# Routing work of batch 6 moved among the last batch's attention steps

## The reference, cut to what matters

```
x = x + tanh(g_xattn[0]) * retention(layernorm(x), ctx)          # stages F (front)
x = x + tanh(g_ffn[0])   * (relu(x W_up) W_down + expert mix)     # stages F
x = x + tanh(g_xattn[1]) * attention(layernorm(x), ctx, ctx)      # stages T, for the last batch L
x = x + tanh(g_ffn[1])   * (shared(x) + top 6 of 64 experts(x))   # stages R route, then the experts

# attention: 8 batches, 8 heads of 32 x 512
sm  = softmax(einsum('bdm,bdn->bmn', qh, kh) * scale)
ret = einsum('bmn,bcn->bcm', sm, vh)
# last layer, for each token:
scores = sigmoid(layernorm(x) @ w_gate); top 6; weights; position in the expert's queue (CAP 256)
```

## Time and profile before

| | us |
|---|---|
| median of 3 runs | 1052.45 |
| lowest, highest of them | 1051.8, 1053.76 |
| the profiled execution | 1051.3 |
| its span, first to last instruction | 1049.5 |
| PE busy in it | 990.5 |
| DVE, ACT, POOL busy | 603.0, 335.0, 465.1 |

### The profile page before, as it was taken

The page is one execution under the profiler, slowest core; times in us unless marked ns, Lnnn a source line. Parts: engine busy times, 40 slices in busy tenths (PEclk is TensorE's granted clock), DMA queues, the critical chain, the costliest instruction groups (busy, mean ns, idle before and its releaser), DMA issues.

```text
span 1049.5 us, 15353 instructions
## 1 busy us (share of the span) xinstructions
PE 990.5 (94%) x5629; PEld 603.6 (58%) x5630; DVE 603.0 (57%) x1249; ACT 335.0 (32%) x491; POOL 465.1 (44%) x457
## 2 busy tenths in 40 slices
PE   7999989999999999999999998895999999999886
PEld 6986545564564564464465452344777777776432
DVE  3334554765765855746756747543655556553566
ACT  3411024124133233323333231442444434443221
POOL 2000025526557467477467544352355555556000
PEclk9999999999999999999999999898999999999999
DMA  8793279697680590680610409356899999965998
GB/s 321 284 385 127 103 256 332 222 357 293 232 327 28 209 336 1 234 311 1 238 68 32 152 32 363 153 206 265 303 373 387 371 370 368 371 255 208 380 417 322
DMA packets 93622, 262.23 MB, mean 250 GB/s; under 512 B 10454, under 2 KB 10582, under 8 KB 92784
## 3 DMA queue, kind: packets, MB, share of 16 engines
q1 hardware_dynamic: 43760, 146.18, 38.0%
q10 hardware_dynamic: 31872, 63.97, 16.3%
q0 software_dynamic: 17920, 51.15, 12.4%
HBM read 129.91 MB, written 139.72 MB: 257 GB/s over the span
## 4 chain that ended last, share of the span: by engine, by line
PE 68%; DVE 8%; POOL 7%; DMA 7%; issue 6%; ACT 2%; SPq 0%; POOLq 0%; ACTq 0%; DVEq 0%
PE banks L1273 17%; PE banks L1892 11%; PE banks L1283 10%; DMA e_eo<-y_d 6%; PE banks L1881 6%; PE banks L1901 6%; POOL t_psum L773 5%; PE banks L1391 5%; PE banks L1453 5%; DVE t_nmx L1064 2%; PE banks L1471 2%; ACT t_probs L864 2%; DVE t_nmx L1073 1%; PE banks L1265 1%; PE banks L1456 1%
## 5 line engine op out<-in xcount | busy, mean ns | idle before, releaser
L1715 POOL DMA_INDIRECT y_d<-e_eo,e_ids x128 | 124.5, 973 | 126.3 <-DVE e_eo L1812 93.6
L1064 DVE TENSOR_REDUCE t_nmx<-banks 128x4 f32<-128x2048 f32 x56 | 128.1, 2287 | 58.3 <-PE banks L1391 58.3
L773 POOL TENSOR_TENSOR t_psum<-t_psum,t_probs 128x512 f32<-128x512 f32 x104 | 128.7, 1268 | 61.9 <-ACT t_probs L864 61.0
L864 ACT ACTIVATE t_probs<-banks 128x2048 f32<-128x2048 f32 x56 | 105.2, 1878 | 139.7 <-PE banks L1456 115.8
L785 POOL DMA_INDIRECT xs_d<-r_norm,r_xaddr x96 | 95.9, 998 | 49.2 <-issue 24.9
L1453 PE MATMUL banks<-b_qry,b_key 32*128 32x512 f32 x512 | 73.9, 647 | 7.9 <-ACT t_probs L864 5.7
L743 POOL TENSOR_TENSOR f_rstd<-f_veps,mhalf 128x2 f32<-128x2 f32 x24 | 16.8, 699 | 144.2 <-DVE f_veps L962 144.2
L1881 PEld LDWEIGHTS banks<-ident,e_xg 128*128 128x128 f32 x512 | 56.9, 143 | 34.3 <-issue 34.1
L1881 PE MATMUL banks<-ident,e_xg 128*128 128x128 f32 x512 | 63.9, 280 | 12.5 <-DMA e_xg<-xs_d 12.5
L773 POOL TENSOR_TENSOR t_psum<-t_probs,t_probs 128x512 f32<-128x512 f32 x52 | 66.5, 1316 | 12.4 <-ACT t_probs L864 6.3
L1391 PE MATMUL banks<-b_key,b_qry 32*128 32x512 f32 x448 | 63.9, 639 | 3.7 <-DVE t_nmx L1064 2.0
(11 more groups left out here) (227 smaller groups left out, 1646.7 us busy)
## 6 DMA issues: line engine op xcount, KB each, us to landing
xs_d<-zero ACTq DMA_DIRECT2D x32, 1056.0 KB, 7.1
e_xg<-xs_d SPq DMA_DIRECT2D x32, 1056.0 KB
y_d<-zero ACTq DMA_DIRECT2D x24, 1024.0 KB, 7.5
e_xg<-y_d SPq DMA_DIRECT2D x16, 768.0 KB, 14.8
e_eo<-y_d SPq DMA_DIRECT2D x16, 768.0 KB, 14.4
wo<-in_wud SPq DMA_DIRECT2D x6, 768.0 KB, 11.9
wupT<-in_wud SPq DMA_DIRECT2D x6, 768.0 KB, 11.7
a_x<-in_x SPq DMA_DIRECT2D x8, 512.0 KB, 4.7
```

The lines of the kernel that those rows point to most:

```text
L773: ins = g_.tensor_tensor(psum0[:, q, :], first[:, q, :], probs[s % NP][:, q, :], ALU.add)
L864: A(probs[s % NP][:, :, :], quad[:, :, :], ACT.Exp, scale=SCALE1).then_inc(W["exp_ok"], 1)
L1064: V.tensor_reduce(nmx[g][:, m, :], quad[:, :, :], axis=AX.X, op=ALU.max, negate=True).then_inc(W["mx_ok"], 1)
L1715: g_.indirect_dma_start(out=y_d, out_offset=bass.IndirectOffsetOnAxis(ap=ids[:, HC * p + n:HC * p + n + 1], axis=0), in_=eo[u][:, n, :], i ...
```

## The change

The table `ENDING` has the routing of batch 6 at other places, two entries of `CHOSEN` go, so that `R.turnA/6` and `R.turnB/6` take work banks of the rotation instead of pV's and a chosen one, and the first `L.V` of batch 7 waits for the copy of `L.up0` (the last user of pV's bank now) instead of for that of `R.turnA/6`. No instruction is added or removed.

- `R.stats/6` and `R.norm/6` stood ahead of the maxima of `L.S5` and of `L.S7`; they stand behind `L.P1/7` on DVE.
- `R.turnA/6`, `R.turnB/6` stood ahead of `L.Q0/7`; they stand behind `L.V0/7`.
- `R.gates/6` stood behind `L.Q0/7`; it stands behind `L.V1/7`. `R.pos/6` stood behind `L.Q2/7` and `L.M1/7`; it stands behind `L.V2/7`.
- `L.Q1/7` stands directly behind `L.Q0/7`.

```diff
-L.S1b/7 L.S2/7 L.V6/6 L.V7/6 T.cT/7 T.A1/6 L.up0a/7 T.add1/6 R.x1/5 L.S3a/7 L.S4/7 L.S3b/7 L.up0b/7 L.P0/7 R.x2/5 R.stats/6 L.S5/7 L.S6a/7 L.M0/7 L.up0c/7 L.up0d/7
-R.norm/6 L.S7/7 L.S6b/7 R.turnA/6 R.turnB/6 R.x3/5 R.acc/5 R.acc/6 L.P1/7 L.Q0/7 R.gates/6 R.keep/6 L.Q1/7 L.V0/7 R.top/6 L.Q2/7 L.M1/7 R.pos/6 L.V1/7 L.Q3/7
...
+L.S7/7 L.S6b/7 R.x3/5 R.acc/5 R.acc/6 L.Q0/7 L.P1/7 R.stats/6 R.norm/6 L.Q1/7 L.V0/7 R.turnA/6 R.turnB/6 L.Q2/7 L.M1/7 L.V1/7 R.gates/6 R.keep/6 L.Q3/7 R.top/6
+L.V2/7 R.pos/6 R.slots/6 R.x0/6 R.weigh/6 R.x1/6 R.x2/6 L.Q4/7 L.V3/7 L.A0/7 L.add0/7 L.stats0/7 R.x3/6 L.Q5/7 L.V4/7 L.norm0/7 L.Q6/7 L.V5/7 L.turn0/7 L.Q7/7 L.gates0/7 L.top0/7
...
-CHOSEN = {("L.V4", 6): 2, ("L.up0a", 7): 3, ("L.M0", 7): 2, ("R.turnA", 6): 3, ("R.turnB", 6): 2}
+CHOSEN = {("L.V4", 6): 2, ("L.up0a", 7): 3, ("L.M0", 7): 2}
...
-                    pe.wait_ge(W["x4T_ok"], 2 * b - 1)
+                    pe.wait_ge(W["raw_ok"], 1)
```

More of the change, by code:

```diff
@@ L449 @@
 F.down0/7 T.sum0c/6 T.Q5/6 F.down1/7 T.Q6/6 T.V3/6 T.Z0/6 T.Q7/6 F.stats3/7 R.x3/4 F.norm3/7 T.A0/6 L.V4/6 L.S0/7 L.S1a/7 L.V5/6 T.add0/6 R.x0/5
-L.S1b/7 L.S2/7 L.V6/6 L.V7/6 T.cT/7 T.A1/6 L.up0a/7 T.add1/6 R.x1/5 L.S3a/7 L.S4/7 L.S3b/7 L.up0b/7 L.P0/7 R.x2/5 R.stats/6 L.S5/7 L.S6a/7 L.M0/7 L.up0c/7 L.up0d/7
-R.norm/6 L.S7/7 L.S6b/7 R.turnA/6 R.turnB/6 R.x3/5 R.acc/5 R.acc/6 L.P1/7 L.Q0/7 R.gates/6 R.keep/6 L.Q1/7 L.V0/7 R.top/6 L.Q2/7 L.M1/7 R.pos/6 L.V1/7 L.Q3/7
-R.slots/6 R.x0/6 R.weigh/6 L.V2/7 R.x1/6 R.x2/6 L.Q4/7 L.V3/7 L.A0/7 L.add0/7 L.stats0/7 R.x3/6 L.Q5/7 L.V4/7 L.norm0/7 L.Q6/7 L.V5/7 L.turn0/7 L.Q7/7 L.gates0/7 L.top0/7
+L.S1b/7 L.S2/7 L.V6/6 L.V7/6 T.cT/7 T.A1/6 L.up0a/7 T.add1/6 R.x1/5 L.S3a/7 L.S4/7 L.S3b/7 L.up0b/7 L.P0/7 R.x2/5 L.S5/7 L.S6a/7 L.M0/7 L.up0c/7 L.up0d/7
+L.S7/7 L.S6b/7 R.x3/5 R.acc/5 R.acc/6 L.Q0/7 L.P1/7 R.stats/6 R.norm/6 L.Q1/7 L.V0/7 R.turnA/6 R.turnB/6 L.Q2/7 L.M1/7 L.V1/7 R.gates/6 R.keep/6 L.Q3/7 R.top/6
+L.V2/7 R.pos/6 R.slots/6 R.x0/6 R.weigh/6 R.x1/6 R.x2/6 L.Q4/7 L.V3/7 L.A0/7 L.add0/7 L.stats0/7 R.x3/6 L.Q5/7 L.V4/7 L.norm0/7 L.Q6/7 L.V5/7 L.turn0/7 L.Q7/7 L.gates0/7 L.top0/7
 L.V6/7 L.pos0/7 L.slots0/7 L.rows0a/7 L.V7/7 L.up1/7 L.A1/7 L.up2/7 L.add1/7 L.stats1/7 L.rows0b/7 L.norm1/7 L.turn1/7 L.gates1/7 L.top1/7 L.pos1/7 L.slots1/7 L.rows1/7
```

## The result

The changed kernel takes 1066.36 us (median of 4, 1064.57 to 1067.76) against 1052.22: ratio 1.0135, interval 1.0113 to 1.0158. That is slower, as forecast, but 14 us instead of 4.8, and outside the range. A second measurement of the same kernel gave 1063.57 us and 1.0114 (1.0092 to 1.0136). The profiled execution is the slowest of the first four: 1067.76 us, span 1066.0.

What follows compares the result with a forecast made beforehand. PE, busy 94% of the span, was taken as the bound, beside a path through POOL's queue with 0.74 us to spare. 1.6 + 1.7 + 1.5 = 4.8 us on 1052.45 gave 1057.3 us, range 1053.8 to 1060.0 (8 in 10).

Steps and rivals of the forecast that it cites:

- the maxima's gain at `L.Q0`: On DVE, moments and norm leave the maxima: `L.Q0` starts at 662.4 us against 664.71, a gain of 2.3 us.
- the positions' lateness: PE reaches the positions of batch 6 at 678.3 us, so its addresses are out at 679.7, 2.3 us later.
- the gap ahead of L1503: PE stands idle for 4.6 us ahead of the turn of the last batch's first half.
- The rival in which PE alone sets the end: POOL's rows do not gate the turn, PE's gain of 2.9 us goes through: 1049.5 us; chance of faster 0.04.
- that in which the clock never falls: Gaps of 2.0 and 4.6 us on PE leave the clock alone, only +1.6 us remains: 1054.1 us; chance 0.17.
- step 6: PE's clock falls to half near `L.Q1` and ahead of the turn, priced at 1.7 and 1.5 us.
- the first fall: Half clock on PE around 667 to 670 us, costing between nothing and 3.4 us; the middle, 1.7, was taken.
- step 2: On PE from `L.Q0` to the gates: 2.0 us idle ahead of `L.Q1`, gates end at 675.1 us, 6.25 us later.
- Step 5: POOL's nine row DMAs, 11.18 us, stand ahead of the root; the turn on PE moves by +1.6 us.
- the second fall: Half clock on PE from the idle ahead of the turn, bounds 0 and 3.4 us; 1.5 was taken.
- The experts' start: Its first microseconds run at half clock as well, so it can add or give back some 1 us.
- the cases named as slower: Falls at both places at a middle price 0.43, one fall 0.27, both long 0.07; slower was given 0.75.

Runs made afterwards that it cites:

- a_roots: Changed kernel with six of batch 6's nine row DMAs behind the root of `L.stats0`, and the last batch's first rows behind that of `L.stats1`: 1054.69 us, ratio 1.0024.
- a_fillturn: Changed kernel with five unread products on PE in the gap ahead of the turn of the last batch's first half: 1059.39 us, ratio 1.0078.
- a_up1: a_roots with the shared product `L.up1` cut in two halves, put ahead of and behind `L.Q0` instead of behind `L.V7`: 1053.07 us, ratio 1.0009.
- b_roots: Kernel before with three of the nine row DMAs behind the root of `L.stats0`, and the last batch's first four rows behind that of `L.stats1`: 1053.47 us, ratio 1.0021.
- a_gates: Changed kernel with only gates and positions of batch 6 earlier, the gates directly behind `L.Q2`, the positions ahead of `L.Q3`: 1056.43 us, ratio 1.0046.
- b_fillx: Kernel before with twelve unread products on PE while it waits for the experts' rows: 1051.27 us, ratio 0.9997.

## Why the prediction was wrong

Right were the direction and its mechanism: the maxima's gain at `L.Q0` (2.25 us for 2.3), the hole of 2.0 us behind it, the positions' lateness, POOL's nine rows ahead of the root, the gap ahead of L1503 (5.1 for 4.6), and half clock at both places. The rival in which PE alone sets the end is refuted by `a_roots` and `a_fillturn`; that in which the clock never falls by the clock rows.

What failed is step 6, the price of the clock: both falls were priced at a middle, and the second under a bound that did not hold. With it the sum failed in its sizes, term by term:

1. *Step 6, the first fall.* I took 1.7 of at most 3.4 us. The half clock lasted 6.8 us, all of it on the path of the addresses: 3.4. The gates end 36.25 us after the mark, which is the 33.0 of my step 2 and 3.3 more. My reason for the middle, that weighings bring the clock back soon, was read from one case.
2. *Step 5, the nine rows.* 11.77 us instead of 11.18, since one issue took 1.47 us and the first 1.04: 0.6. The turn is 5.5 us late in the trace: 1.6 + 3.3 + 0.6.
3. *Step 6, the second fall.* I took 1.5, and set 3.4 as the bound because the first stretch of half clock in the trace of before had cost no more. It lasted 10.2 us and cost 4.26 (11.04 less 6.78, `a_fillturn`). A bound taken from another event is no bound.
4. *The experts' start,* which I had put at 1 us either way. Half clock until 744.9, 4.9 us into the experts' work instead of 3.1, and from their first transposes to the end 1.8 us longer (326.0 for 324.2). That the longer half clock did it is not shown: in `a_up1` it ended 3.1 us into this work, and the stretch took 325.7 us all the same.
5. *The reference.* Between them these give 9.96 + 1.8 = 11.8 us against the profiled execution of before. That execution had the fall near 667, which other executions of this order do not have. Against those (80.82 + 324.4) it is 14.0 us. The two measurements, 14.1 and 11.8 us, lie at these two ends. Step 6 says that only 1.1 us of that fall lay on the path of the addresses before. That reading was wrong: in `b_roots` they are out at 32.45 us, 2.82 earlier than in the trace that I worked from, because `L.Q1` and `L.V0`, ahead of the positions on PE, stood at half clock, too.

Three slips moved nothing in the sum: step 5 has 690.65 where its rows give 690.60, the remark behind step 6 has 666.97 for 666.94, and the chances of the cases named as slower add up to 0.77, not 0.75.

The first and third terms hang together, and that was the larger mistake. I gave the two falls prices as if they were drawn apart from the waits, where the runs show a chain: the holes on PE bring half clock, this makes the gates and so the addresses late, POOL's nine rows behind them widen the gap ahead of the turn, the clock falls again in that gap, and the rest is late. `a_gates` shows the gain of breaking it early: 2.84 us at the addresses, 7.53 at the experts. With two such links the sum belonged at the full price of both, not at a middle.

## What to carry to other kernels

When an engine's wait is removed ahead of a stage that alternates between two engines, look at what stood in its holes: here the gates of batch 6 lay where PE waited for exponentials, and taking them out gave back the 2.25 us as a hole of 2.03 at once. Ask what stands in the queue behind a late input; nine indirect DMAs of 1.3 us each turned a lateness nobody waited for into a stall, and putting the short instruction that others wait for ahead of six of them took away 9 of 10 us. Price a new gap of several microseconds on PE as the gap and a stretch at half clock behind it, at its full length: here 5.1 us of gap and 4.3 more. Where work is moved into a hole, look at what it had covered where it stood: `L.up1` left a wait of 2.1 us behind.

## What the runs showed of the hardware

- The half clock comes and goes between executions of one program: the kernel before ranged from 1048.0 to 1054.4 us over the runs made here, and the mark in the four traces of its order by 4.1 us. A single profile of either kernel says which falls are possible, not which there will be.
- A gap of 1.26 us on PE (`a_gates`) left the clock alone. In one of 5.10 us the clock fell after 4.1 us and stayed at half for 10.2 us, although PE was busy again from 701.6 on. Behind the holes of 1.58 and 2.03 us it was 6.8 us, and 3.4 us with fillers in the second.
- Filling the gap of 5.1 us with unread products kept the clock: 6.78 us for the same work that took 11.04 (`a_fillturn`). Ahead of the experts it kept the clock as well and brought nothing, since PE waited for rows there (`b_fillx`).
- One indirect row DMA takes POOL 1.28 us from issue to issue, 0.97 of it busy; one in nine took 1.47 us here.
